# Attention outputs turned by transposing DMAs, and z turned one slot sooner

## What is computed

```python
q = einsum(x, Wq, Wt) + bt                    # 4 groups x 12 heads x 64, per token
q = gelu(q)
q = layernorm(q) * gt + betat                 # over the 64 of a head
qf = concat([relu(q), relu(-q)]) / sqrt(128)
out = einsum('gbhnd,bhdm->gbhnm', qf, kv)     # kv, ksum: per batch and head, made before
out = out / (einsum(qf, ksum) + 1e-6)
out = out.reshape(b, n, 4 * 768)
fused = gelu(layernorm(out @ Wf + bf) * gf + betaf)   # Wf: 3072 x 768
h = h + fused @ Wo + bo
```

## Time and profile before

| what | value |
|---|---|
| time, median of 3 runs | 2499.05 us (2498.91 to 2499.41) |
| the profiled execution | 2497.05 us, span 2495.3 us |
| busy: PE, DVE, ACT, POOL | 2370.7, 2038.6, 1839.3, 1292.9 us |
| mean granted clock of PE | 0.984 |
| the loop of `attend` | from 706 to 2435 us, 40 tiles, 42.52 us each in its middle |
| DMA, whole program | 46.28 MB; next to nothing after the first third |

### The profile page before, as it was taken

One profiled execution on the slowest core, in us unless ns is written; L12 is line 12 of the kernel. 1 busy time (PEld: TensorE's weight loads), 2 busy tenths in 40 slices (PEclk: granted clock), 3 DMA queues, 4 the chain that ended last, 5 costly groups with the idle time before them and its releaser, 6 DMA issues. The chain is left out here.

```text
span 2495.3 us, 61438 instructions
## 1 busy us (share of the span) xinstructions
PE 2370.7 (95%) x22026; PEld 1669.4 (67%) x22026; DVE 2038.6 (82%) x3219; ACT 1839.3 (74%) x2892; POOL 1292.9 (52%) x1253
## 2 busy tenths in 40 slices
PE   5999999899989999999999999999999999999985
PEld 3777776666656666666666666766666666666654
DVE  7999999878867878787878787878878787878755
ACT  6777777566667777778777878787777778777854
POOL 0000000256666666666666666666666666666660
PEclk9999999999989999999999999999999999999997
DMA  6421111111100000000000000000000000000002
GB/s 142 127 58 38 38 45 31 35 52 44 51 13 2 1 0 0 0 0 0 0 0 0 0 0 0 0 0 0 0 0 0 0 0 0 0 0 0 0 1 64
DMA packets 21800, 46.28 MB, mean 19 GB/s; under 512 B 5684, under 2 KB 12340, under 8 KB 21428
## 3 DMA queue, kind: packets, MB, share of 16 engines
q1 hardware_dynamic: 20596, 45.06, 7.0%
q10 hardware_dynamic: 1152, 0.51, 0.1%
HBM read 41.62 MB, written 3.93 MB: 18 GB/s over the span
## 5 line engine op out<-in xcount | busy, mean ns | idle before, releaser
L1091 ACT ACTIVATE phi<-ps_t,betat,gt 64x512 f32<-64x512 f32 (+1 forms) x1280 | 852.2, 666 | 17.1
L1338 POOL TENSOR_TENSOR phi_lo<-phi 128x512 bf16<-128x512 f32 x480 | 515.4, 1074 | 550.4 <-ACT phi L1091 550.4
L1018 PE MATMUL ps_y<-staging,o_hi 128*128 128x384 bf16 x1920 | 468.7, 326 | 21.7 <-DVE o_lo L1208 21.7
L1018 PE MATMUL ps_y<-staging,o_lo 128*128 128x384 bf16 x1920 | 468.9, 326 | 0.0
L1018 PE MATMUL ps_y<-wf_lo,o_hi 128*128 128x384 bf16 x1920 | 468.9, 326 | 0.0
L1330 POOL TENSOR_TENSOR q_ssq<-q_ssq,half 128x8 f32<-128x8 f32 x240 | 439.2, 1830 | 18.8
L1208 DVE TENSOR_TENSOR o_lo<-ps_u,o_hi 128x512 bf16<-128x512 f32 x240 | 164.4, 685 | 213.9 <-ACT o_hi L1101 213.9
L172 PE MATMUL acc<-w_b,feat 128*128 128x384 bf16 x1728 | 295.5, 331 | 34.2 <-ACT feat L223 28.1
L1101 ACT ACTIVATE o_hi<-ps_u 128x512 bf16<-128x512 f32 x240 | 143.5, 598 | 239.3 <-PE ps_u L1004 239.3
L1018 PEld LDWEIGHTS ps_y<-staging,o_lo 128*128 128x128 bf16 x1920 | 187.9, 98 | 124.2
L1018 PEld LDWEIGHTS ps_y<-wf_lo,o_hi 128*128 128x128 bf16 x1920 | 187.7, 98 | 124.3
(11 more groups left out here) (268 smaller groups left out, 5427.9 us busy)
## 6 DMA issues: line engine op xcount, KB each, us to landing
xt<-in_x_dram SPq DMA_DIRECT2D x32, 320.0 KB, 5.2
ex_big<-in_wf_dram SPq DMA_DIRECT2D x24, 384.0 KB, 3.2
xt<-in_x_dram SPq DMA_DIRECT2D x32, 256.0 KB, 5.7
out_dram<-h SPq DMA_DIRECT2D x8, 480.0 KB, 4.6
staging<-in_wq_t_dram SPq DMA_DIRECT2D x1, 3072.0 KB, 12.6
staging<-in_tok_w_dram SPq DMA_DIRECT2D x8, 240.0 KB, 10.4
staging<-in_tok_w_dram SPq DMA_DIRECT2D x8, 192.0 KB, 10.3
staging<-in_kv_w_dram SPq DMA_DIRECT2D x1, 1536.0 KB, 15.8
```

What stands on the lines that cost most here:

```text
L1018: last = nc.tensor.matmul(ps_y[:, n, 0:HC], lhs, w[part][:, c, n * HC:(n + 1) * HC], start=c == 0 and lhs is oh and part == 'wf_hi', stop= ...
L1091: last = nc.scalar.activation(phi[sign * DH:(sign + 1) * DH, j % 2, a:b, head, :], ps_t[rows, a * P:b * P].rearrange("p (i n) -> p i n", n ...
L1338: nc.gpsimd.tensor_tensor(phi_lo[:, j % 2, :, head], phi[:, j % 2, :, head], phi_hi[:, j % 2, :, head], ALU.subtract).then_inc(s["phi_lo_d ...
```

## The change

The four transposes of the outputs on PE (`turn_outputs`) and their bank `ps_u` go. `high_outputs` and `low_outputs` now read `o` in SBUF and write the bf16 halves side by side into `oh`; SP issues one transposing DMA per octet from `oh` to `ot`, and `fuse` takes its operands from `ot`, one slot later than before (octet j-3). `ps_t` gets the freed bank, and `turn_octet` turns z of octet j+1 at the end of slot j, behind the fusing products, in place of octet j after the queries. The tile's later steps (`move_y`, statistics, `turn_y`, `fused_gelu`, `low_ys`, `project_out`, `add_to_h`) move one slot with it. `divide` now waits for both halves of the octet before, `high_outputs` for the DMA of two octets before, `fuse` for its DMA. `xn`, `xl` and `xe` lie in spare columns of other tiles, and one semaphore of the experts' constants is joined with another.

```diff
@@ -795,17 +796,16 @@
...
         ys_hi = y.bitcast(BF16)[:, 1::2]
         sq = flat[:, RING * OC + INNER:RING * OC + INNER + OC].rearrange("p (h d) -> p h d", h=OCT)
-        xn = sb("xn3", [P, 2 * P], F32)
+        xn = flat[:, RING * OC + INNER + OC:]
         xh = sb("xh3", [P, 2, P], BF16)
-        xl = sb("xl3", [P, P], BF16)
-        xe = sb("xe3", [P, P], BF16)
+        xl, xe = (ex['spare'][:, n * P:(n + 1) * P] for n in range(2))
         z = sb("z", [P, 2, OCT, DH], F32)
         phi = sb("phi", [P, 2, PAIRS, 2, P], F32)
...
         phi_lo = sb("phi_lo", [P, 2, PAIRS, 2, P], BF16)
         o = sb("o", [P, 2, PAIRS, DH], F32)
-        o_hi = sb("o_hi", [P, 2, OC], BF16)
-        o_lo = sb("o_lo", [P, 2, OC], BF16)
+        oh = sb("o_halves", [P, 2, 2, OC], BF16)
+        ot = sb("o_turned", [P, 2, 2, PAIRS, P], BF16)
         ys_lo = sb("ys_lo", [P, INNER], BF16)
         total = sb("q_sum", [P, 2, OCT], F32)
...
@@ -815,20 +815,20 @@
...
 
         ps_a = ctx.enter_context(nc.psum_tensor("ps_a", [P, 2, 512], F32))
-        ps_t = ctx.enter_context(nc.psum_tensor("ps_t3", [P, 512], F32))
+        ps_t = ctx.enter_context(nc.psum_tensor("ps_t3", [P, 2, 512], F32))
         ps_o = ctx.enter_context(nc.psum_tensor("ps_o", [P, 2, 512], F32))
-        ps_u = ctx.enter_context(nc.psum_tensor("ps_u", [P, 512], F32))
         ps_y = ctx.enter_context(nc.psum_tensor("ps_y", [P, 2, 512], F32))
 
...
                  "queries gelu_done q_sum centered squared q_ssq_s q_var q_rstd q_scaled "
                  "q_turned phi_done phi_lo_done attended den_done rec_done o_done "
-                 "o_turned o_hi_done o_lo_done fused y_moved y_bn_s y_aggr y_var y_rstd y_norm "
+                 "o_hi_done o_lo_done fused y_moved y_bn_s y_aggr y_var y_rstd y_norm "
                  "y_turned ys_done ys_lo_done out_proj h_part h_done "
-                 "ex_zero ex_const ex_in ex_bn ex_aggr ex_kept ex_var ex_root ex_sum ex_steps").split()
+                 "ex_zero ex_const ex_in ex_bn ex_aggr ex_kept ex_var ex_root ex_steps").split()
         s = {n: sem("at_" + n) for n in names}
-
-        USES = ("oct3", "oct4", "oct5", "x", "oct0", "oct1", "f0", "f1", "oct2", "r")
+        turned = [sem(f"at_o_turned{n}") for n in range(2)]
+
+        USES = ("oct3", "r", "oct4", "oct5", "x", "oct0", "oct1", "oct2", "f0", "f1")
         bank = {n: k % 2 for k, n in enumerate(USES)}
 
...
@@ -897,7 +897,9 @@
...
             if use == "x":
                 return tile.next(), [("xe_ready", 0, 1), ("xl_ready", 0, 1)]
-            return tile.prev(), [("h_part", 0, 1)] if use == "r" else [("ys_done", int(use[1:]), 2)]
+            if use == "r":
+                return tile.prev().prev(), [("h_part", 0, 1)]
+            return tile.prev(), [("ys_done", int(use[1:]), 2)]
 
         def free_bank(eng, tile, use):
...
@@ -942,6 +944,17 @@
...
                 sp.wait_ge(s["ex_in"], 16 * 20)
 
+                def turn_outputs(tile, j):
+                    sp.wait_ge(s["o_lo_done"], count(tile, j, NO))
+                    if (n := earlier(tile, j, NO, 2)) is not None:
+                        sp.wait_ge(s["fused"], n)
+                    sp.dma_start(ot[:, j % 2].rearrange("p k i n -> p (k i) n"),
+                                 oh[:, j % 2].rearrange("p k c -> p (k c)"), transpose=True).then_inc(turned[j % 2], 16)
+
+                for t in range(TILES):
+                    for j in range(NO):
+                        turn_outputs(Tile(t), j)
+
             @block.tensor
             def _(pe):
...
@@ -969,11 +982,11 @@
...
                 def turn_octet(tile, j):
                     pe.wait_ge(s["q_scaled"], count(tile, j, NO))
-                    if (n := earlier(tile, 2 * j, 2 * NO, 1)) is not None:
+                    if (n := earlier(tile, 2 * j, 2 * NO, 3)) is not None:
                         pe.wait_ge(s["phi_done"], n)
                     for i in range(PAIRS):
                         last = nc.tensor.transpose(
-                            ps_t[:, i * P:(i + 1) * P],
+                            ps_t[:, j % 2, i * P:(i + 1) * P],
                             z[:, j % 2, 2 * i:2 * i + 2].rearrange("p h d -> p (h d)"), ident[:, :])
                     last.then_inc(s["q_turned"], 1)
...
@@ -995,29 +1008,18 @@
...
                     last.then_inc(s["attended"], 1)
 
-                def turn_outputs(tile, j):
-                    pe.wait_ge(s["o_done"], count(tile, j, NO))
-                    if (n := earlier(tile, j, NO, 1)) is not None:
-                        pe.wait_ge(s["o_hi_done"], n)
-                        pe.wait_ge(s["o_lo_done"], n)
-                    for i in range(PAIRS):
-                        last = nc.tensor.transpose(ps_u[:, i * P:(i + 1) * P],
-                                                   o[:, i // 2, 2 * (i % 2):2 * (i % 2) + 2].rearrange("p h d -> p (h d)"), ident[:, :])
-                    last.then_inc(s["o_turned"], 1)
-
                 def fuse(tile, j):
-                    pe.wait_ge(s["o_hi_done"], count(tile, j, NO))
-                    pe.wait_ge(s["o_lo_done"], count(tile, j, NO))
+                    pe.wait_ge(turned[j % 2], 16 * count(tile, j // 2, NO // 2))
                     if j == 0 and (n := earlier(tile, 0, 1, 1)) is not None:
                         pe.wait_ge(s["y_moved"], n)
                     for i in range(PAIRS):
                         c = PAIRS * j + i
-                        oh, ol = (v[:, j % 2, i * P:(i + 1) * P] for v in (o_hi, o_lo))
-                        for lhs, part in ((oh, 'wf_hi'), (oh, 'wf_lo'), (ol, 'wf_hi')):
+                        hi, lo = (ot[:, j % 2, k, i, :] for k in range(2))
+                        for lhs, part in ((hi, 'wf_hi'), (hi, 'wf_lo'), (lo, 'wf_hi')):
                             for n in range(2):
                                 last = nc.tensor.matmul(ps_y[:, n, 0:HC], lhs, w[part][:, c, n * HC:(n + 1) * HC],
-                                                        start=c == 0 and lhs is oh and part == 'wf_hi',
-                                                        stop=c == PAIRS * NO - 1 and lhs is ol)
+                                                        start=c == 0 and lhs is hi and part == 'wf_hi',
+                                                        stop=c == PAIRS * NO - 1 and lhs is lo)
                     last.then_inc(s["fused"], 1)
 
...
@@ -1045,25 +1047,24 @@
...
                     if j == 2 and tile.next().real:
                         turn_x(tile.next(), tile)
-                    if j == 4 and tile.prev().real:
+                    if j == 5 and tile.prev().real:
                         turn_y(tile.prev(), 0, tile)
-                    if tile.real:
-                        turn_octet(tile, j)
                     of, k = octet(tile, j - 1)
                     if of.real:
                         attend_octet(of, k)
-                    if j == 4 and tile.prev().real:
+                    if j == 5 and tile.prev().real:
                         turn_y(tile.prev(), 1, tile)
-                    of, k = octet(tile, j - 2)
+                    of, k = octet(tile, j - 3)
                     if of.real:
                         fuse(of, k)
-                    of, k = octet(tile, j - 1)
+                    of, k = octet(tile, j + 1)
                     if of.real:
-                        turn_outputs(of, k)
-                    if j == 5 and tile.prev().real:
-                        project_out(tile.prev(), tile)
+                        turn_octet(of, k)
+                    if j == 0 and tile.prev().prev().real:
+                        project_out(tile.prev().prev(), tile)
 
                 all_slots(pe, slot)
+                project_out(Tile(TILES - 1), Tile(TILES + 1))
 
             @block.scalar
...
@@ -1090,15 +1091,16 @@
...
                                 last = nc.scalar.activation(
                                     phi[sign * DH:(sign + 1) * DH, j % 2, a:b, head, :],
-                                    ps_t[rows, a * P:b * P].rearrange("p (i n) -> p i n", n=P), ACT.Relu,
+                                    ps_t[rows, j % 2, a * P:b * P].rearrange("p (i n) -> p i n", n=P), ACT.Relu,
                                     bias=w['betat'][rows, sign, g:g + 1], scale=w['gt'][rows, sign, g:g + 1])
                         last.then_inc(s["phi_done"], 1)
 
                 def high_outputs(tile, j):
-                    act.wait_ge(s["o_turned"], count(tile, j, NO))
-                    if (n := earlier(tile, j, NO, 2)) is not None:
-                        act.wait_ge(s["fused"], n)
-                    nc.scalar.activation(o_hi[:, j % 2], ps_u[:, 0:OC], ACT.Copy).then_inc(s["o_hi_done"], 1)
+                    act.wait_ge(s["o_done"], count(tile, j, NO))
+                    if (n := earlier(tile, j // 2, NO // 2, 1)) is not None:
+                        act.wait_ge(turned[j % 2], 16 * n)
```

(51 more changed lines are left out.)

## The result

The changed kernel takes 2413.55 us (median of 4 runs, 2412.32 to 2414.01) against 2498.98 us before on the same chip: 85.4 us less, a ratio of 0.9658 with a 95% interval of 0.9641 to 0.9674. The forecast was 2390, with a range of 2374 to 2580.

The account below looks back on a forecast made before the run. PE's queue plus 0.50 us of waiting bounds a tile: 42.52 - 2.61 - 0.50 + 0.27 = 39.68 us. Forty tiles save 113.6, less 5 for ends 108.6: about 2390 us, own range 2376 to 2405, stated 2374 to 2580.

Parts of the forecast that it names:

- rival A: The transposing DMA outlasts its 6.1 us window; slower than before from 7.7 us, about 2690 us at 10; chance 0.16.
- rival B: DVE becomes the bound around slot 3, PE waiting 0.5 to 1 us a tile: 2405 to 2435 us; chance 0.10.
- What bounds the kernel: In the attention loop, a tile costs what PE's queue costs plus 0.50 us of waiting, 42.52 us measured.
- Removed turns: Four fp32 transposes per octet leave PE's queue: 104.4 us, or 2.61 a tile, all on the path.
- The DMA: One transposing DMA per octet on SP's queue, taken as 4.5 us, costing nothing up to about 6 us.
- the case of rows of 256 B: The transposing DMA moves 1024 packets: 0.9 us on 16 engines plus about 2.3, so 3.3 us.
- runs of 32 B: The DMA's turned side is written in 16-element runs, 8192 packets: 7.5 us plus 2.3, about 10.
- A': The DMA's eight blocks go one after another, 10 us or more per octet: about 3320 us; chance 0.08.
- z one slot sooner: In slot 3 z takes 5.6 or 6.2 us against PE's 6.15: 0.06 us; with the GELU bank's 0.2, 0.27 a tile.
- the wait that goes: PE's wait for the low half in front of the fusing products disappears, 0.50 us a tile.
- DVE's new low half: low_outputs reads SBUF twice in place of PSUM: 0 to 0.35 us more on 240 octets, taken as 0.2.
- The ends: The pipeline is one slot deeper, so fusing products and DMA stand alone at the end: 4 to 6 us, taken as 5.

Follow-up runs that it names:

- e3: Changed kernel with every octet's transposing DMA issued twice, the second after the first has landed: 2415.74 us.
- e4: Changed kernel with every octet's transposing DMA issued three times, each after the one before has landed: 2725.03 us.
- e1: Changed kernel with low_ys ahead of the experts' row roots in POOL's slot 0, in place of behind them: 2400.07 us.
- e5: Changed kernel with z turned in its old place, octet j in slot j ahead of attending, second bank kept: 2406.01 us, ratio to before 0.9634.
- e8: Changed kernel with low_ys ahead of the row roots on POOL and z turned in its old place: 2393.32 us.
- e2: Changed kernel without the transposing DMAs, fusing products reading the halves unturned from three buffers (computes something else): 2412.31 us.

## Why the prediction was right, and where it was off

The time lies inside the stated range, but that range was wide, because it reached into rival A. The forecast's own range of 2376 to 2405 was missed by 8.6 us, and 2413.55 lies where rival B was priced (2405 to 2435), whose cause did not come about in that size. The profiled spans show where the miss arose: 108.6 us were forecast and 83.1 came. Forty tiles at the measured 2.64 us are 105.7 in place of 113.6, which leaves 22.6 for the ends in place of 5.

**What bounds the kernel:** right. A tile costs PE's queue plus its waits, before and after; taking 2.61 us out of the queue and 0.66 of waiting, and adding 0.63 of new waits, took 2.64 us off the tile.

**Removed turns, 2.61 us a tile:** right. In the changed kernel a slot without extras is turn, queries, attending, fusing: 6.2 us from turn to turn (1376.34 to 1382.55), the wait for z included, where it was 6.59.

**The DMA:** right in kind, and better than the value taken. It landed after 3.0 us, not 4.5, in 1056 packets an octet (1024 of 256 B and 32 of 4 B), so the case of rows of 256 B, priced at 3.3, was the true one; there are no runs of 32 B. Rivals A and A' did not come about. e3 shows that 6.1 us are free and e4 that 9.3 are not. The issue takes 1.23 us on SP, and the packets of one DMA lie within 1.42 us, about 185 GB/s. Of the two statements of the Trainium skill, this is nearer to that of "DMA: Bandwidth & Descriptors", section on latency and other measured facts (261 GB/s, by which 256 KB are estimated to move in 1.0 us), though slower. By the other, of the Trainium skill's "VectorE: DVE Perf Modes", section on the three transpose paths (1309 ns for one block), eight blocks one after another are estimated at 10.5 us, and the whole 256 KB land in 3.0; what one block alone takes, no run here shows.

**z one slot sooner:** the place was right, the price was not. In slot 3 z was done 6.15 us after the fusing products that release DVE (1376.34 to 1382.49), having met POOL, the upper of the two values given:

```profile
1376.54 0.96 DVE L1216 TENSOR_TENSOR shared<-ps_y,bf 128x768 f32<-128x768 f32 x1 [0.45 <-PE ps_y L1020]
...
1380.91 1.04 POOL L1339 TENSOR_TENSOR phi_lo<-phi 128x512 bf16<-128x512 f32 x1 [2.04 <-ACT phi L1092]
...
1381.14 1.35 DVE L1186 TENSOR_TENSOR z<-shared,q_ssq 128x512 f32<-128x512 f32 x1
```

PE's load for the turn waited 0.29 us, of which 0.13 cost PE time, where 0.06 was counted. The wait for the GELU's bank was 0.30 and more, where 0.2 was counted, and a third one of 0.14 for `phi_lo` had not been seen. Read from PE's starts, everything above the nominal steps was 0.67 us a tile before, of which I had counted 0.50 as the wait that goes; so 0.44 was forecast for after, and 0.64 came. Two errors stand behind that, and they partly cancel. The wait that goes was in truth 0.66 (attending to fusing took 1428.57 to 1429.96 in the earlier trace rows, 1.39 in place of 0.73), and the new waits are 0.63 in place of 0.27. That is the 0.2 us a tile, 8 us in all, by which the loop is above the forecast: rival B, well below the size it was given.

**DVE's new low half:** right. Its mean is 797 ns against 685, 0.11 more, between the bounds of 0 and 0.35; z and centering changed by -115 and +91 ns beside it.

**The ends, 5 us:** this is the term that failed; it was 22.6. The step of the prediction that is wrong is the one on POOL: "`low_ys` moves in front of `low_phi` of slot 0, 1.5 us on an engine with 14 us free". That counted the loop and forgot that in the last slot 0 another step of POOL's queue, the row roots, stands ahead of it; e1 shows 13.5 us for it. The other part is the start: the sentence on z looked at the loop, where PE comes to z after fusing products, and not at the first slots, where there are none; e5 shows 4.3 us. With both put right, in e8, the span is 102.4 us below before, where forty tiles at its 2.69 us are 107.8: the ends then cost 5.4, about the 5 that the forecast gave them.

Of the 9.8 us by which the first `move_y` is later, 3.5 more lie in the stage. They are near the 3.9 of one slot of fusing products, but the granted clock from 720 to 740 us is also lower (0.67 against 0.83 before), and no run separates the two. The last 2.0 arose ahead of the stage, in code that is the same. The stage's first transposes of x start anywhere from 706.2 to 708.9 us in the ten traces of kernels with the change, so 2.0 is within what one execution differs from another.

## What to carry to other kernels

When a step is moved, walk its new queue through the first and the last iterations too: a step that is free in the loop can land behind work that exists only once. A long wait of PE there costs more than its length, since the products behind it ran at the lower clock (11.9 us of waiting, 2.9 of slower work). A step that waits for something late should stand behind work that is ready, and while a pipeline fills there may be none. And when several waits of 0.1 to 0.3 us lie close together, removing one shows the next; try them in combination before one is called worthless.

## What was not expected of the hardware

A transposing DMA of 128 x 1024 bf16 within SBUF lands in 3.0 us, 1.23 us of it the issue on SP, next to a plain 256 KB load's 2.6. Over one tile of the loop, 39.87 us, the queue of the changed kernel shows (packets, MB, share of 16 engines):

```profile
q1 hardware_dynamic: 6336, 1.57, 21.0%
```

That is 0.21 x 16 x 39.87 us / 6336 = 21 ns of engine time a packet, against the 14.6 of the earlier trace rows, and e2 found no effect of it on any other engine.
